# Kept blocks of the mask in DRAM, and one head's rows turned by VectorE and ScalarE, in a four-layer graph kernel

## The reference, cut to what matters

```
h = relu(layernorm(x)); x = x + L0(h, adj)     # weighted mean over a row of adj, times W, + b, relu
h = relu(layernorm(x)); x = x + L1(h, adj)     # attention, two heads (i = 0, 1)
h = relu(layernorm(x)); x = x + L2(h, adj)     # attention, one head
h = relu(layernorm(x)); x = x + L3(h, adj)     # adj.T @ h over the column sums
# L1, for each head i:
mask = (adj > 0) | eye(n)
h = x_norm @ ff0_w[i].T
e = where(mask, leaky_relu(s_src[:, None] + s_dst[None, :]), NEG)
att = layernorm(softmax(e) @ h + x) * g2 + b2
h_next += elu(att @ ff1_w[i].T) / 2
# L2: the same kind of softmax, but with mask = adj > 0 (no eye)
```

## Time and profile before

| | us |
|---|---|
| median of 3 runs (lowest, highest) | 1197.39 (1197.26, 1198.12) |
| span of the profiled execution | 1195.6 |
| median less that span: what lies around it | 1.8 |
| TensorE busy (PE) | 1190.9 |
| VectorE busy (DVE) | 939.5 |
| ScalarE busy (ACT) | 301.6 |

### The profile page before, as it was taken

How to read it: one execution, slowest core, us unless ns; L and a number is a source line. 1 busy time by engine, 2 the same in 40 slices (tenths; PEclk the granted TensorE clock), 3 DMA queues, 4 the chain that set the end, 5 groups by cost and what they waited for, 6 DMA issues and landing times.

```text
span 1195.6 us, 16808 instructions
## 1 busy us (share of the span) xinstructions
PE 1190.9 (100%) x6299; PEld 823.9 (69%) x6299; DVE 939.5 (79%) x1704; ACT 301.6 (25%) x732; POOL 10.0 (1%) x21
## 2 busy tenths in 40 slices
PE   9999999999999999999999999999999999999999
PEld 9999999965444444444554547999999974444455
DVE  5448675798978787889788797798787869886886
ACT  3312122235323242422333144541212121000000
POOL 3000000000000000000000000000000000000000
PEclk9999999999999999999999999999999999999999
DMA  9888888700111102110000000022303068999830
GB/s 324 295 269 293 295 292 302 254 25 8 46 18 36 18 35 35 53 18 18 1 18 0 18 1 19 2 90 106 141 0 141 1 261 305 310 334 319 320 86 18
DMA packets 79284, 153.18 MB, mean 128 GB/s; under 512 B 35456, under 2 KB 44016, under 8 KB 79216
## 3 DMA queue, kind: packets, MB, share of 16 engines
q1 hardware_dynamic: 53264, 145.43, 34.8%
q10 hardware_dynamic: 25456, 6.30, 2.4%
q0 software_dynamic: 496, 0.55, 0.2%
HBM read 144.33 MB, written 4.24 MB: 124 GB/s over the span
## 4 chain that ended last, share of the span: by engine, by line
PE 98%; DVE 1%; ACT 0%; issue 0%; DVEq 0%
PE acc L504 51%; PE acc L488 37%; PE acc L761 4%; PE mix L570 1%; PE mix L557 1%; PE mix L542 1%; PE turn L519 1%; PE acc L769 1%; DVE ring L1323 0%; PE turn L515 0%; PE mix L628 0%; ACT V L788 0%; DVE U L1454 0%; PE turn L638 0%; PE mix L645 0%
## 5 line engine op out<-in xcount | busy, mean ns | idle before, releaser
L1323 DVE SCALAR_TENSOR_TENSOR ring<-G,score,mask 128x1024 f32<-128x1024 f32 x372 | 467.0, 1280 | 76.5 <-PE acc L504 42.9
L504 PE MATMUL acc<-ring,G 128*128 128x512 f32 x1000 | 436.2, 593 | 0.2 <-DVE acc L1263 0.2
L504 PEld LDWEIGHTS acc<-ring,G 128*128 128x128 f32 x1000 | 186.7, 190 | 227.0 <-issue 213.4
L488 PE MATMUL acc<-G,ring 128*128 128x129 f32 x2240 | 253.8, 275 | 0.0
L488 PEld LDWEIGHTS acc<-G,ring 128*128 128x128 f32 x2240 | 252.0, 192 | 0.8 <-issue 0.8
L488 PE MATMUL acc<-G,mask 128*128 128x129 f32 x1648 | 186.2, 275 | 0.0
L488 PEld LDWEIGHTS acc<-G,mask 128*128 128x128 f32 x1648 | 185.0, 192 | 0.0
L504 PE MATMUL acc<-mask,G 128*128 128x512 f32 x384 | 165.8, 593 | 0.0
L1597 DVE TENSOR_TENSOR ring<-ring,mask 128x1024 f32<-128x1024 f32 x120 | 146.8, 1223 | 10.7
L504 PEld LDWEIGHTS acc<-mask,G 128*128 128x128 f32 x384 | 72.6, 190 | 90.9 <-issue 89.7
L1361 DVE TENSOR_SCALAR mask<-mask 128x1024 uint8<-128x1024 f32 x103 | 68.5, 689 | 38.0 <-DMA mask<-in_adj_t 37.6
(11 more groups left out here) (210 smaller groups left out, 692.9 us busy)
## 6 DMA issues: line engine op xcount, KB each, us to landing
mask<-in_adj SPq DMA_DIRECT2D x128, 512.0 KB, 5.5
mask<-in_adj_t SPq DMA_DIRECT2D x103, 512.0 KB, 4.9
ring<-in_adj_t SPq DMA_DIRECT2D x18, 512.0 KB, 5.0
G<-given_rows SPq DMA_DIRECT2D x10, 512.0 KB, 3.9
G<-in_adj_t SPq DMA_DIRECT2D x4, 512.0 KB, 5.3
inputs<-V ACTq DMA_DIRECT2D x4, 512.0 KB, 2.7
V<-inputs SPq DMA_DIRECT2D x4, 512.0 KB, 3.9
X<-in_x SPq DMA_DIRECT2D x3, 512.0 KB, 8.6
```

The costliest lines, as they stand in the source:

```text
L488: mm = pe.matmul(acc[:, b, (s % 3) * DW:(s % 3) * DW + DW], lhs[:, s * P:(s + 1) * P], g, start=(k == 0 and s % 3 == 0), stop=(k == T - 1) ...
L504: mm = pe.matmul(acc[:, c, :], g, moving[:, c * BANK:(c + 1) * BANK], start=(k == 0), stop=(k == T - 1), skip_group_check=True)
L1323: dve.scalar_tensor_tensor(slots[k % L], late_home[h] if early and k >= EARLY else rows_home[h, q], rank[h][:, k:k + 1], span(mask, (q * T ...
```

## The change

- The own blocks of each quarter are copied from the mask to a DRAM tensor before `self_loops` changes them (`keep_own`, issued by SyncE before tile 12 of the next quarter of pass 0, the last one at the end of the pass), and copied back behind the last tile of that quarter in head 2 (`return_own`). VectorE's pattern steps and the load of the diagonal are gone. VectorE waits for `own_kept` before `self_loops` and for `own_back` before a quarter of pass 3.
- The sums of quarters 0 to 2 of head 2 are turned by one VectorE block transpose into `turn` and by 16 ScalarE instructions of 32 partitions x 256 elements, which put each block of 32 x 32 on its partitions and apply g2 and b2 on the way. TensorE's `turned` step is left out there. Quarter 3 stays as it was.
- The steps stand behind other tiles: VectorE's `half`, `rest`, `scal` behind 6, 7, 8 (before: 8, 10, 11, and 6, 8, 10 in the last quarter), the block transpose behind 11; TensorE's `apply` behind 14, and in the last quarter behind 13 (before: 14 and 12).

```diff
-    WEIGHTS = 15
+    WEIGHTS = 14
+        given_blocks = nc.dram_tensor("given_blocks", (P, T * P), U8, kind="Internal").ap()
+        def own_blocks(q):
+            start = q * (T + S) * QC
+            before = QC if q == Q - 1 else 0
+            there = mask[:, start - before:start - before + S * (QC + P)].rearrange("p (s c) -> p s c", c=QC + P)[:, :, before:before + P]
+            return there, given_blocks[:, q * S * P:(q + 1) * S * P].rearrange("p (s c) -> p s c", c=P)
+            def keep_own(q):
+                sp.wait_ge(mask_made, (q + 1) * T)
+                there, here = own_blocks(q)
+                sp.dma_start(here, there).then_inc(own_kept, 16)
+            def return_own(q):
+                sp.wait_ge(e_made, (Q + q + 1) * T)
+                sp.wait_ge(own_kept, 16 * Q)
+                there, here = own_blocks(q)
+                sp.dma_start(there, here).then_inc(own_back, 16)
             def layer0(q, some=range(T)):
                 for k in some:
+                    if q > 0 and k == 12:
+                        keep_own(q - 1)
...
+            keep_own(Q - 1)
             sp.wait_ge(own_made, Q)
...
             bring_back(0)
-            bring_back(1)
-            bring_back(2)
-            bring_back(3)
+            for q in range(1, Q):
+                return_own(q - 1)
+                bring_back(q)
+            return_own(Q - 1)
...
-                return (sums_back, apply) if h == 0 else (sums_back, turned, apply)
+                return (sums_back, apply) if h == 0 or not last_of(q) else (sums_back, turned, apply)
...
                 if last_of(q):                                   # TensorE, stage2
-                    ks = [1, 11, 12, 25, 26, 28, 29]
+                    ks = [1, 13, 25, 26, 28, 29]
                 else:
-                    ks = [0, 12, 14, 27, 28]
+                    ks = [0, 14, 27, 28]
...
+            def widen_blocks(got, n, done, scale_, bias_):
+                act.wait_ge(got, n)
+                for i in range(P // 32):
+                    for d in range(P // 32):
+                        rows = slice(32 * d, 32 * d + 32)
+                        src = turn[32 * i:32 * i + 32, :].rearrange("p (s d r) -> p s d r", d=4, r=32)[:, :, d, :]
+                        dst = U[rows, 0:QC].rearrange("p (s i r) -> p s i r", i=4, r=32)[:, :, i, :]
+                        ins = act.activation(dst, src, ACT.Identity, bias=bias_[rows, :], scale=scale_[rows, :])
+                ins.then_inc(done, 1)
...
-                    widen(n_turned, q + 1, n_wide, g2c, b2c)
+                    (widen if fixed(q) and q == Q - 1 else widen_blocks)(n_turned, q + 1, n_wide, g2c, b2c)
...
+                if h == 3:                                       # VectorE, run
+                    dve.wait_ge(own_back, 16 * (q + 1))
...
                 def self_loops():
-                    dve.wait_ge(mask_made, (q + 1) * T)
+                    dve.wait_ge(own_kept, 16 * (q + 1))
...
+                def turn_in_blocks():
+                    dve.wait_ge(n_norm, j + 1)
+                    dve.wait_ge(f_wide, q + Q + 1)
+                    dve.transpose(turn[:, :], flat_v).then_inc(n_turned, 1)
+                turns = [small_turns] if h == 0 else [turn_in_blocks] if q < Q - 1 else []
...
                 if last_of(q):                                   # VectorE, stage2
-                    ks = [4, 4, 6, 8, 10, 17, 17, 12, 14, 19, 21, 24, 28, 30, 30]
+                    ks = [4, 4, 6, 7, 8, 11, 17, 17, 19, 21, 24, 28, 30, 30]
                 else:
-                    ks = [4, 5, 8, 10, 11, 19, 19, 12, 15, 20, 22, 23, 28]
+                    ks = [4, 5, 6, 7, 8, 11, 19, 19, 20, 22, 23, 28]
```

More of the change, by code:

```diff
@@ L119, in graph_layers @@
         zero = sb("zero", [P, S])
-        dsub = sb("dsub", [P, T])
         centre = ring[:, 0, 0:P]
@@ L199, in graph_layers @@
         consts_made, dve_step = sem("consts_made"), sem("dve_step")
+        own_kept, own_back = sem("own_kept"), sem("own_back")
         affine_made, back_summed, back_placed = sem("affine_made"), sem("back_summed"), sem("back_placed")
@@ L466, in _ @@
             loads = [(bias0_b, bias0.partition_broadcast(P)), (alphac, alpha.partition_broadcast(P)),
-                     (w2raw, w2_t), (attnc[:, 0:4], attn), (attnc[:, 4:6], a2), (dsub[:, :], diag),
+                     (w2raw, w2_t), (attnc[:, 0:4], attn), (attnc[:, 4:6], a2),
                      (back_w[0][:, 0:D], ff0_t[0]), (back_w[1][:, 0:D], ff0_t[1])]
@@ L1368, in prepare @@
                 dve.wait_ge(consts_made, 2)
-                dve.tensor_scalar(restc, alphac, -1.0, 1.0, ALU.mult, ALU.add)
-                st.mark(dve.tensor_scalar(dsub[:, :], dsub[:, :], 0.0, -1.0, ALU.is_gt, ALU.add))
+                st.mark(dve.tensor_scalar(restc, alphac, -1.0, 1.0, ALU.mult, ALU.add))
                 dve.wait_ge(qv_summed, 1)
@@ L1484, in add @@
                     dve.wait_ge(post_done, n + 1)
[L1486 to L1498, removed]
                 def small_turns():
@@ L1501, in small_turns @@
                     dve.transpose(flat, V[:, :, :].rearrange("p s d -> p (s d)")).then_inc(small_turned, 1)
-                turns = [small_turns] if h == 0 else []
-                steps = [residual, residual_rest] + statistics(lambda s: U3[:, s, 0:D], n_var) + [scal] + turns + [elu, add]
-                return steps if h == 0 else steps + [own_pattern, own_pattern_rest]
+                def turn_in_blocks():
[3 more added lines that the diff above has]
+                turns = [small_turns] if h == 0 else [turn_in_blocks] if q < Q - 1 else []
+                return [residual, residual_rest] + statistics(lambda s: U3[:, s, 0:D], n_var) + [scal] + turns + [elu, add]
             def late_steps(h):
@@ L1559, in _ @@
             last = post1(1, Q - 1)
-            ks = [3,4,5,7,8,14,14,14,16,17,21,22,23,24,25,27,30,31]
-            run(3, 0, at(ks, last[:-2] + feed(3, 4 * Q - 1, Q - 1) + late_steps(3) + [mean_of_all, keep_mean]
-                         + [last[-2], last[-1]]))
+            ks = [3,4,5,7,8,14,14,14,16,17,21,22,23,24,25,27]
+            run(3, 0, at(ks, last + feed(3, 4 * Q - 1, Q - 1) + late_steps(3) + [mean_of_all, keep_mean]))
             def post2(q):
```

## The result

| | before | changed |
|---|---|---|
| median (lowest to highest) of 6 runs each | 1197.94 us (1197.26 to 1198.12) | 1202.1 us (1201.2 to 1202.45) |
| ratio, 95% interval | | 1.0035, 1.0025 to 1.0045 |
| span of the profiled execution | 1195.6 us | 1200.6 us |

The changed kernel is 4.2 us slower. 1196.8 had been forecast, within 1194.8 to 1199.8.

A forecast was written before the change was run, and what follows sets the result against it. TensorE's own stream was taken to bound the kernel. Quarters 1 and 2 of pass 2 gain 1.74 us, quarter 3 loses 1.15, the rest zero: 1197.39 - 0.6 = 1196.8 us, 8-in-10 range 1194.8 to 1199.8.

The forecast's parts named there:

- TensorE alone bounds the kernel, and an edit pays only in its stream: Whole kernel: 98% of the span is TensorE's own work; an edit gains only what it removes there, costs only TensorE's waits.
- forecast 2.75 for that case: Pass 2, copies quick enough that quarter 3 does not wait: -2.75 us, 1194.6 us in all; chance 0.09.
- VectorE's steps packed closer: Pass 2, quarters 1 and 2: VectorE never waits before the block transpose, reaches it at 562.0 and takes 1.24 us.
- The sixteen copies, 7.7 us: ScalarE's copies after the block transpose: 0.475 us a step, 7.7 us for all sixteen, ends 6.3 and 10.9.
- Rival B: ScalarE's copies do not overlap: 0.58 us each, 9.3 in all, kernel +2.2 us, 1199.6; chance 0.14.
- break-even of 8.3 us: Duration of the sixteen ScalarE copies from which the changed kernel is slower than before.
- No wait in quarters 1 and 2, -1.74 us: Pass 2: U ready 0.9 us before TensorE reaches `apply`, so both quarters keep their full 0.87 us gain.
- Quarter 3, +1.15 us: Last quarter of pass 2: TensorE waits 2.1 us for the copies before `apply`, so the quarter loses 1.15 us.
- The 0.14 us that `apply` lost in quarter 3 before: Old kernel, pass 2: `apply` takes 1.93 us instead of 1.78, read as already waiting 0.14 us for ScalarE.
- The kept blocks at zero, their waits at zero: Eight added DMAs of own mask blocks and the new waits on them: no cost, with 6.9 us of cover in pass 0.
- Rival C: Pass 0: small writes hold up the loads beyond 6.9 us, +4 us, 1200.8; chance 0.05.
- The table of the Trainium skill that sends such a transpose to TensorE: Head 2's 128 x 128 transpose: the rule prefers TensorE into PSUM, since VectorE covers only 32 x 32 blocks; by it the change loses.

## Why the prediction was wrong

- *TensorE alone bounds the kernel, and an edit pays only in its stream:* right. With the copies in time the gain was 2.76 us, forecast 2.75 for that case.
- *VectorE's steps packed closer:* right within 0.1 us. The block transpose started 0.4 us after the forecast in quarter 1, which is the profile's later start, and at 1.25 us for 1.24.
- *The sixteen copies, 7.7 us:* wrong, the term that failed first. They took 9.1 us, a step of 0.57 for 0.475. The overlap that the forecast counted on was not there. Its step was taken from rows of instructions that all use the same 128 partitions, and for these it was a little long: sixteen of 128 x 256 took 7.40 us (L74), a constant shift 7.23 and 7.29. That the series on its own partitions took 7.66, nearly the forecast's 7.7, is luck: twelve of its steps are 0.45 and three are 0.57. That copies of 32 partitions cost nothing more was written down as assumed. Rival B, at a chance of 0.14, had the right mechanism, no overlap, and 9.3 us; its reason was "writes to other partitions than were read", and the runs put in its place a change of partitions from one instruction to the next. The forecast's break-even of 8.3 us was passed.
- *No wait in quarters 1 and 2, -1.74 us:* wrong by that term. The margin of 0.9 us was smaller than the 1.4 by which the copies were longer. TensorE waited 0.57 us in each and paid 0.27 more in `apply`, so that nothing of the 0.87 was left. Measured -0.05 us.
- *Quarter 3, +1.15 us:* the wait was to be 2.1 us and was 3.65, for the same 1.4 and 0.1 of earlier steps. But there the sum also had no term for what a wait does to TensorE afterwards: it gave `apply` 1.79 us at once and the tiles behind it their old pace. They took 1.55 us more in `apply` and 0.36 behind it, some 1.65 for the half clock and 0.27 for the first products. Measured 4.18 + 0.36. With 9.1 us of copies and no such term the forecast's own sum gives about +1.6 us in all (-0.46 in each of quarters 1 and 2, +2.55 in quarter 3), 1199.0, inside the range. So the copies alone turn the forecast's gain into a loss; what follows a wait, 1.9 us in quarter 3 and 0.27 in each of the other two, put the time outside the range.
- *The 0.14 us that `apply` lost in quarter 3 before:* read as a wait. The rows have ScalarE done with U at 692.14 + 1.45 = 693.59, 0.17 before TensorE comes at 693.76. U came too late for the weight load to be covered; it is a small case of the same 0.27, and the sum did not carry it over to the steps that would wait.
- *The kept blocks at zero, their waits at zero:* right within the 1 us that the run of the kept blocks alone can tell. Rival C did not come about.
- *The table of the Trainium skill that sends such a transpose to TensorE* ("VectorE: DVE Perf Modes", Rules for kernel authors) would have had the better answer for the kernel as it was laid out, but not for the reason of delay as such: with the same delay and `apply` behind tile 15 the new path wins.

## What to carry to other kernels

When work is moved off the bounding engine, what counts is the delay of the new path against the point at which the bounding engine comes for it; price the longest link from a row with the same pattern of partitions, or measure it alone, before choosing that point. A wait of TensorE can cost more than its length, here 1.9 us beyond the 3.65 of the wait: look at the granted clock behind it, and move the waiting step back by one tile rather than let it wait. If a step is late by a margin near your uncertainty, leave one tile more; here that cost 0.18 us a quarter, and nothing once VectorE's statistics stood later too.

## What the runs showed of the hardware

- ScalarE overlaps neighbouring instructions (0.545 us for one, 0.45 a step) in these series only when both the set of partitions that is read and the one that is written stay the same; a change of either brings the step to 0.57. A constant shift costs nothing (sixteen in 7.29 and 7.23 us). "ScalarE: Activation LUTs" of the Trainium skill, What ACT_TABLE_LOAD costs, gives back-to-back instructions an overlap of about 93 ns without this condition; the series agree where the partitions stay and not where they change.
- TensorE's granted clock was 1.00 through a wait of 3.7 us, fell to 0.50 about 0.5 us behind it, stayed there some 3.4 us and cost some 1.65 us. With the loops swapped the same wait had it fall before its end, at a cost of 1.4. It did not fall in the profile with waits of 0.6 and 1.96 us; two of that kernel's eleven runs were 2 us longer with a mean granted clock of 0.999 instead of 1.000.
- The first products behind a wait took 2.05 us for sixteen instead of 1.78, at full clock, even when the wait was only 0.57 us. The first weight load then starts with the end of the wait (572.92), where before it ran 0.59 us ahead of the first product.
